# A four-layer triangle kernel on one core: the turned picture is stored in bands of eight rows from 128 partitions, and four pairs of filler products in layer 0 are left out

## What is computed

```python
x = x + L0(gn(x)); x = x + L1(gn(x)); x = x + L2(gn(x)); x = x + L3(gn(x))
# one layer, on its normalised input xn (layers 0 to 2 normalise each position first)
left  = (xn @ Wl) * mask * sigmoid(xn @ Wlg)
right = (xn @ Wr) * mask * sigmoid(xn @ Wrg)
t     = einsum('bikd,bjkd->bijd', left, right)   # layers 0 and 1: along rows
t     = einsum('bkjd,bkid->bijd', left, right)   # layers 2 and 3: along columns
out   = layernorm(t) * sigmoid(xn @ Wog) @ Wout  # each layer has its own order of gate and Wout
```

## Time and profile before

| | us |
|---|---|
| median of three runs | 1471.77 (1465.33 to 1473.02) |
| the profiled execution, its own time | 1468.82 |
| its span on the core | 1466.6 |
| TensorE busy | 1268.9 (87%) |
| VectorE busy | 1006.8 (69%) |
| ScalarE busy | 932.2 (64%) |
| GpSimd busy | 528.5 (36%) |

### The profile page before, as it was taken

How to read it: one execution, slowest core, us unless ns; L and a number is a source line. 1 busy time by engine, 2 the same in 40 slices (tenths; PEclk the granted TensorE clock), 3 DMA queues, 4 the chain that set the end, 5 groups by cost and what they waited for, 6 DMA issues and landing times. The chain is left out here.

```text
span 1466.6 us, 43428 instructions
## 1 busy us (share of the span) xinstructions
PE 1268.9 (87%) x12854; PEld 769.3 (52%) x12854; DVE 1006.8 (69%) x2880; ACT 932.2 (64%) x2045; POOL 528.5 (36%) x490
## 2 busy tenths in 40 slices
PE   0799998899799998999950999999899788899898
PEld 0455554577454544765530555557555343467564
DVE  6577776388699996219970788852299899921687
ACT  0577775599577774229960788851499677722675
POOL 0355552045455553004530666630055300000355
PEclk9999999999899999999985999999999899999999
DMA  8011113578433332986659455549799544469797
GB/s 286 22 50 52 50 48 97 154 221 253 155 109 107 107 112 73 285 270 188 193 147 222 153 185 165 176 136 299 243 277 282 182 154 150 145 208 312 236 300 251
DMA packets 219684, 258.74 MB, mean 176 GB/s; under 512 B 53984, under 2 KB 208992, under 8 KB 219360
## 3 DMA queue, kind: packets, MB, share of 16 engines
q1 hardware_dynamic: 185504, 227.18, 49.9%
q10 hardware_dynamic: 34112, 30.68, 7.4%
HBM read 139.83 MB, written 117.96 MB: 176 GB/s over the span
## 5 line engine op out<-in xcount | busy, mean ns | idle before, releaser
L1062 DVE SCALAR_TENSOR_TENSOR lr<-ps,mask,act_out 128x128 f32 (+5 forms) x1152 | 278.8, 310 | 52.9 <-ACT act_out L805 46.5
L1232 POOL TENSOR_TENSOR rstd<-ve,half_col 128x6 f32<-128x6 f32 x144 | 190.3, 1322 | 254.8 <-DVE ve L1029 221.1
L1277 POOL TENSOR_TENSOR new_ring<-val,lr 128x384 f32<-128x384 f32 x96 | 103.4, 1077 | 386.6 <-issue 303.1
L568 PE MATMUL ps<-w_parts,val 64*128 64x256 bf16 (+1 forms) x1728 | 199.1, 309 | 18.9 <-DVE lr L1062 18.1
L805 ACT ACTIVATE act_out<-ps 128x384 f32<-128x384 f32 x384 | 176.0, 483 | 50.3 <-PE ps L578 34.1
L1265 POOL TENSOR_TENSOR val<-act_out,gate_ring 128x384 f32<-128x384 f32 x96 | 103.6, 1080 | 225.1 <-ACT act_out L882 186.0
L781 ACT ACTIVATE cen<-ps,gn 128x384 f32<-128x384 f32 x144 | 83.8, 582 | 102.0 <-PE ps L523 99.6
L859 ACT ACTIVATE cen<-ps 128x384 f32<-128x384 f32 x192 | 108.5, 565 | 61.9 <-PE ps L678 61.6
L678 PE MATMUL ps<-in_ring,k 128*128 128x384 f32 x288 | 130.3, 536 | 17.5 <-DMA in_ring<-t_scratch 17.2
L1113 DVE COPY cen<-ps 128x384 f32<-128x384 f32 x48 | 26.8, 558 | 160.6 <-PE ps L636 160.6
L636 PE MATMUL ps<-lr 64*128 64x192 f32 (+3 forms) x896 | 125.5, 330 | 8.8 <-DVE lr L1062 5.2
(11 more groups left out here) (112 smaller groups left out, 2595.5 us busy)
## 6 DMA issues: line engine op xcount, KB each, us to landing
gate_scratch<-gate_ring SPq DMA_DIRECT2D x192, 192.0 KB, 2.3
gate_ring<-gate_scratch SPq DMA_DIRECT2D x96, 384.0 KB, 3.7
lr<-x_scratch SPq DMA_DIRECT2D x72, 384.0 KB, 5.1
in_ring<-t_scratch SPq DMA_DIRECT2D x144, 192.0 KB, 3.4
x_scratch<-new_ring SPq DMA_DIRECT2D x48, 384.0 KB, 3.2
in_ring<-x_scratch SPq DMA_DIRECT2D x96, 192.0 KB, 2.4
lr<-x SPq DMA_DIRECT2D x6, 1536.0 KB, 15.9
t_scratch<-cen SPq DMA_DIRECT2D x96, 96.0 KB, 4.0
```

The costliest lines, as they stand in the source:

```text
L568: mm = nc.tensor.matmul(banks[h][:, :, 0:P], moving(x, s)[half(h), N * r:N * r + P], proj_weights(w, h)[:, 0:2 * P], start=start, stop=sto ...
L1062: ins = nc.vector.scalar_tensor_tensor(out5[:, h, lo // 2:hi // 2, :, m], ps[:, 4 + 2 * r + h, lo:hi].rearrange("p (a e) -> p a e", e=2), ...
L1232: nc.gpsimd.tensor_tensor(rstd[:, s % 2, :], ve[:, s % 2, :], half_col[:, :], ALU.pow)\
```

## The change

`turned_dram` becomes 24 bands of 128 partitions x 8 rows. SyncE stores band 0 of each half and ScalarE bands 1 to 11 of each half, every DMA from all 128 partitions: two DMAs each in place of four. ScalarE's pieces are 3,072 B long in place of 33,792 B. `gather` reads a band's half of the channels into a half of the partitions, so it becomes four DMAs of 64 partitions in place of two of 128. The counts that wait for these DMAs follow (2 stores, 4 gathers). Apart from that, the two fillers ahead of layer 0's first four output products are gone.

```diff
-EARLY = 4
+BAND = 2 * RING
+BANDS = HALF // BAND
-    turned_dram = nc.dram_tensor("turned_scratch", [2, 2, C, HALF, HALF], F32).ap()
+    turned_dram = nc.dram_tensor("turned_scratch", [2 * BANDS, P, BAND * HALF], F32).ap()
-        def turned_rows(h, h2, first, behind):
-            return (turned_dram[h, h2, :, first:behind, :],
-                    turned[C * h:C * h + C, HALF * h2 + first:HALF * h2 + behind, :])
+        def turned_bands(first, count):
+            bands = turned.rearrange("p (b j) i -> p b (j i)", j=BAND)
+            return (turned_dram.rearrange("b p f -> p b f")[:, first:first + count, :], bands[:, first:first + count, :])
...
-                def gather(n, s):
+                def gather(band, s):
                     for h in range(2):
-                        rows = turned_dram[h].rearrange("h2 c j i -> (h2 c) j i")[:, bass.ds(ROWS * n, 2 * ROWS), :]
-                        slot = in_ring[:, s:s + 2, :].rearrange("p a (r i) -> p (a r) i", r=ROWS)
-                        sp.dma_start(slot[:, :, HALF * h:HALF * h + HALF], rows).then_inc(in_loaded[s], 16)
+                        for h2 in range(2):
+                            rows = turned_dram[bass.ds(BANDS * h2 + band, 1), C * h:C * h + C, ROWS * HALF * s:ROWS * HALF * (s + 2)]
+                            slot = in_ring[C * h2:C * h2 + C, s:s + 2, :].rearrange("p a (r i) -> p (a r) i", r=ROWS)
+                            sp.dma_start(slot[:, :, HALF * h:HALF * h + HALF],
+                                         rows.rearrange("b p (r i) -> p (b r) i", i=HALF)).then_inc(in_loaded[s], 16)
...
-                    sp.wait_ge(in_loaded[s], in_count(l) + 32 * (i + 1))
+                    sp.wait_ge(in_loaded[s], in_count(l) + 64 * (i + 1))
...
-                        gather(n + lead + RING - 1, s - 1)
+                        gather(i + 2, s - 1)
...
                     for h2 in range(2):
-                        for h in range(2):
-                            sp.dma_start(*turned_rows(h, h2, 0, ROWS * EARLY)).then_inc(turned_stored[0], 16)
-                    sp.wait_ge(turned_stored[0], 16 * 4)
+                        sp.dma_start(*turned_bands(BANDS * h2, 1)).then_inc(turned_stored[0], 16)
+                    sp.wait_ge(turned_stored[0], 16 * 2)
...
-                    if l == 0 and isinstance(n, int) and n < RING:
-                        keep_clock(4 + s % 2, 2)
...
                     for h2 in range(2):
-                        for h in range(2):
-                            act.dma_start(*turned_rows(h, h2, ROWS * EARLY, HALF)).then_inc(turned_stored[1], 16)
+                        act.dma_start(*turned_bands(BANDS * h2 + 1, BANDS - 1)).then_inc(turned_stored[1], 16)
```

More of the change, by code:

```diff
@@ L242, in in_count @@
         def in_count(l, s=0):
-            return 16 * TURNS * ((l > 1) + (l > 2) * (2 if s % 2 == 0 else 0))
+            return 16 * TURNS * ((l > 1) + (l > 2) * (4 if s % 2 == 0 else 0))
         n_params = [4 + HAS_LN[l] + (1 if l < 2 else (2 if HAS_MASK[l] else 0)) for l in range(LAYERS)]
@@ L345, in phase_a @@
                     for n in range(0, RING, 2):
-                        gather(n, n)
+                        gather(0, n)
                     for n in range(0, RING, 2):
                         keep(n, 0, n)
-                    sp.wait_ge(turned_stored[1], 16 * 4)
+                    sp.wait_ge(turned_stored[1], 16 * 2)
                     for n in range(0, RING, 2):
@@ L353, in phase_a @@
                         sp.wait_ge(natural_stored[n // 2], 16)
-                        gather(RING + n, n)
+                        gather(1, n)
                     keep(RING, 1, 0)
@@ L516, in centre @@
                     if l == 2:
-                        pe.wait_ge(in_loaded[s // 2 * 2], in_count(l) + 32 * (i + 1))
+                        pe.wait_ge(in_loaded[s // 2 * 2], in_count(l) + 64 * (i + 1))
                     elif l:
@@ L1098, in phase_a @@
                     for part in range(2):
-                        dve.wait_ge(turned_stored[part], 16 * 4)
+                        dve.wait_ge(turned_stored[part], 16 * 2)
                 over_tiles(dve, step)
```

## The result

The changed kernel takes 1504.18 us (median of four runs, 1502.64 to 1507.37) against 1471.74 beside it: a ratio of 1.0232, 95% interval 1.0198 to 1.0266. The forecast was 1449, faster. The profiled execution's span is 1502.1 us, 35.5 more than the earlier trace rows.

The account below looks back on a forecast made before the run. Bound taken: the 60.8 us seam between layers 1 and 2, all on the path, plus layer 0's fillers. 1468.82 - 17.4 - 3.9 = 1447.5 us, or 1450.5 on the median's scale; forecast 1449, midway, range 1438 to 1461.

Parts of the forecast that it names:

- The fillers: Layer 0's second half: removing four filler pairs gains ScalarE's 3.9 us of idle gaps, between 5.9 and a 2 us loss.
- The seam: Between layers 1 and 2: first product at 800.8 in place of 818.19, a gain of 17.4 us.
- the release: Seam: SyncE's second band waits for ScalarE's first DMA, so its gathers are released at 773.0.
- The rival with shorter turns: Seam: queues alternate sooner, SyncE released at 763.2, gain 24.4 + 3.9, 1442 us; chance 0.27.
- The stores: Seam: 9.44 MB from 128 partitions takes 26.1 us against 40.6, all landed at 785.0.
- The stores are not quicker: Rival, seam: stores still end at 798, first product near 814, gain 4.4 + 3.9, 1462 us; chance 0.10.
- The gathers in the loop: Layer 2's 24 pairs: 0.98 us more issue and 1.3 us more transfer fit in 5.3 us of slack, costing nothing.
- Late gathers: Rival, layer 2's loop: half-width gathers take 6.5 us longer and overdraw the slack, 26 us, 1475 us; chance 0.03.
- VectorE's wait: Seam: the wait for both store counts ends at 785.0, products are due at 800.8, so it hides.

Follow-up runs that it names:

- one_pair: The changed kernel with one filler pair put back, ahead of layer 0's tile 0 output product only; 1443.1 us in a single run.
- bands_only: The changed kernel with all four filler pairs put back in layer 0; 1447.84 us, ratio 0.9822.
- lull_fill: The changed kernel with one filler pair put back, ahead of tile 2's spread where TensorE idles; 1442.17 us, ratio 0.9802.
- one_filler: lull_fill with one filler in place of two ahead of tile 2's spread; 1441.75 us in a single run.
- half_piece: lull_fill with bands of four rows in place of eight, so store pieces of 1,536 B; 1445.78 us, ratio 0.9828.
- half_piece_two: half_piece with ScalarE's first two bands of each half stored by DMAs and a count of their own; 1443.64 us, ratio 0.9782.

## Why the prediction was wrong

**The fillers: the step that failed.** The prediction took their 3.9 us as a gain, and bounded the loss by "some 2 us, if TensorE's clock falls to half (1.2 GHz) for a few tiles", one stretch of about 3 us losing half of itself. Mechanism and place were named; the length was not. The fall lasted some 145 us. The stage's output products took 150.5 us from first to last, where at full clock without fillers they take 88.8 (one_pair): the fall cost 61.7 us. Less what the fillers themselves had cost, the last copy came 58.0 us later. The size could have been had: at half clock a tile's work on TensorE takes 3.33 us (the prediction itself had 3.4), more than the 1.95 us a tile of the loop before (382.1 - 290.4 over 47 tiles), so the loop is bound by TensorE at half rate, and 44 tiles to 437 by 1.4 us are some 60 us. What the profile of before could not tell is that the loop doesn't come back by itself. That should have been a rival of its own, with its price of 60 us and its chance.

**The gain itself was real.** Where the clock holds, the removal gives what was forecast. From the first to the last output product of layer 0 are 91.7 us in the kernel before and in bands_only, and 88.6 to 88.8 in one_pair, lull_fill, one_filler and half_piece: 2.9 to 3.1 us for the three pairs that stand between those two products; forecast were 3.9 for four. The last copy comes 2.3 to 4.9 us earlier than in the kernel before in those four kernels (752.49 in one_pair, 755.14 in lull_fill, against 757.42), but not in half_piece_two (757.66), whose clock was at half around 290.

**The seam: right, and under-sized.** Forecast 17.4, measured 25.4. The term that failed is the release: "If a queue keeps its turn for one DMA" gave 15.5, against 7.1. It was read from the first two stretches of the earlier trace rows, in which SyncE's second DMA had hardly started to move, though all four were issued by 763.2: that looks like the late start of the section on the queues, not like a turn. The later row of before shown above has 32 and 32 packets. The rival with shorter turns came within 1 us (24.4), and it had the release at 5.8 and pairs at about 17.5 and 28, against 7.1, 21.5 and 27.5. So its mechanism was nearer, and it deserved more than its 0.27; but that its gain fits so well is in part luck, since it left out the late start (pair 0 came 4 us later) and took 10 us from pair to pair, where 6 were measured.

**The stores: right in kind.** The rate was taken as 361 GB/s from the earlier trace rows, and 399 were measured. "The stores are not quicker" falls: 399 against 221.

**The gathers in the loop: right.** Doubling their number costs nothing that the trace shows: pair 1's wait of 0.99 us is the only one of TensorE's for a gather in the kernel after, and from the first to the last product of the stage are 158.0 us against 157.0. "Late gathers" falls.

**VectorE's wait: right for this kernel.** It shows no wait for the stores in the kernel after. Its cover is thin: with the gathers quicker it is 1.89 us in half_piece and 4.63 in half_piece_two.

**The 2.8 us behind the first product** were not forecast. Up to the last product of the stage 1.0 us of it arises (158.0 against 157.0), in bands_only 2.2 (159.2). The clock there is late: it is 0.50 from 844 to 850 and full only from about 851, when the first product starts, where in the kernel before it is full from about 813, 5 us ahead of it. That this is the cause is likely and not shown; the rest wasn't pursued.

## What to carry to other kernels

A filler that keeps the clock is to be priced by the whole loop behind it: work out what bounds the loop at half clock, multiply by its tiles, and ask what would bring the clock back; and where many fillers stand, take away all but one before taking away all. Here two DMA queues on the same engines passed equal numbers of pieces, so keep the pieces of a large transfer short when a small one is urgent behind it; and reckon with a late start of some us, which shorter pieces did not change. When a stall at a seam goes, follow the same order of work one step past it: here the next count, on which the second gather waited, took back 4 us in full.

## What the runs showed of the hardware

- One loop, with the same instructions, ran steadily at either clock: 89 us at full clock (one_pair) and 150 at half (the kernel after), with TensorE shown as busy 40.00 of 40 us at half. One filler of 0.8 us of work in the right place, or a burst of 6.84 us later, decided which.
- Stores from 128 partitions ran at 399 GB/s over 16 engines, stores from 64 with pieces of the same length at 208.
- Two queues whose pieces moved passed equal numbers of them, at sizes from 384 B to 33,792 B. A gather issued behind a running store moved its first piece 4.6 us later with 128 partitions storing, 7.8 with 64, and 1.2 to 1.4 where the stores were over or nearly over.
- Pieces of 1,536 B cost the stores little: the last had landed at 30.7 us (half_piece); with pieces of 3,072 B it had by 28.5 at the latest (lull_fill).
